# Packing the 88-row remainders of four experts into three full tiles, and writing the gated output over z, in a MoE-Mamba-MoE kernel

## The reference

```
x = x + 0.5 * ffn(layernorm(x))          # FFN 1
x = x + mamba(layernorm(x))              # four Mamba layers, then Wout
x = x + 0.5 * ffn(layernorm(x))          # FFN 2, the same weights

def ffn(xt):                             # 8 experts, 2 of them per token
    topk_w, topk_idx = top_k(xt @ Ws + bs, 2)
    combine = sum(one_hot(topk_idx, 8) * softmax(topk_w))
    g = einsum('td,edf->tef', xt, Wg)    # D = 128, F = 344
    u = einsum('td,edf->tef', xt, Wu)
    y = einsum('tef,efd->ted', silu(g) * u, Wd)
    return einsum('ted,te->td', y, combine)

def mamba_layer(x):                      # 256 channels, 16 states each
    xp, z = split(rmsnorm(x) @ Win)
    xc = silu(causal_conv(xp))           # 4 taps
    dt, B, C = split(xc @ Wx)
    delta = softplus(dt @ Wdt + bdt)
    h[t] = exp(delta[t] * A) * h[t-1] + delta[t] * xc[t] * B[t]
    y = sum_over_states(h * C) + xc * Dp
    return x + (y * silu(z)) @ Wblk
```

## Time and profile before

| | us |
|---|---|
| median of 3 runs | 4566.4 (4564.11 to 4567.35) |
| span of the profiled execution | 4554.2 |
| first core product on POOL | 159.60 |
| last core product on POOL ends | 4402.56 |
| POOL busy | 4093.5 (90%) |
| DVE busy | 4047.9 (89%) |
| PE busy | 3939.2 (86%) |
| ACT busy | 3342.2 (73%) |

### The profile page before, as it was taken

One profiled execution on the slowest core, in us unless ns is written; L12 is line 12 of the kernel. 1 busy time (PEld: TensorE's weight loads), 2 busy tenths in 40 slices (PEclk: granted clock), 3 DMA queues, 4 the chain that ended last, 5 costly groups with the idle time before them and its releaser, 6 DMA issues.

```text
span 4554.2 us, 48397 instructions
## 1 busy us (share of the span) xinstructions
PE 3939.2 (86%) x11712; PEld 1280.3 (28%) x11712; DVE 4047.9 (89%) x5505; ACT 3342.2 (73%) x5047; POOL 4093.5 (90%) x1804
## 2 busy tenths in 40 slices
PE   7886777998999999899998999999899989678769
PEld 2221222232322323232232323223232323122223
DVE  2668898999999999999999999999999999889963
ACT  4566776777777777777778777777777777667734
POOL 0559999999999999999999999999999999999960
PEclk9897887999999999999999999999999999789969
DMA  2233544354434444544454445444444554444410
GB/s 72 61 78 95 115 106 98 85 118 110 97 87 112 107 93 99 114 104 96 98 112 96 97 101 119 95 97 101 112 92 89 117 113 91 101 99 95 99 41 5
DMA packets 154562, 434.46 MB, mean 95 GB/s; under 512 B 16429, under 2 KB 53230, under 8 KB 153903
## 3 DMA queue, kind: packets, MB, share of 16 engines
q1 hardware_dynamic: 154287, 431.36, 41.4%
HBM read 150.28 MB, written 12.58 MB: 36 GB/s over the span
## 4 chain that ended last, share of the span: by engine, by line
POOL 41%; issue 16%; DVE 14%; PE 12%; ACT 8%; DMA 3%; SPq 2%; DVEq 0%; ACTq 0%; POOLq 0%
POOL work L909 21%; POOL work L900 19%; DVE work L720 5%; DVE dA_ps L720 4%; SPq L363 2%; PE d_ps L434 2%; PE s_ps L481 2%; DVE work L725 2%; DMA bc_sb<-bc_rows 2%; ACT sg_sb L583 2%; ACT L583 1%; PE b_ps L427 1%; ACT dA_ps L556 1%; DMA dd_sb<-dd_src 1%; ACT L584 1%
## 5 line engine op out<-in xcount | busy, mean ns | idle before, releaser
L909 POOL TENSOR_TENSOR work<-dd_sb,bc_sb 128x2048 f32<-128x2048 f32 x512 | 2319.6, 4531 | 72.4 <-DMA dd_sb<-dd_src 72.2
L556 ACT ACTIVATE dA_ps<-dd_sb,a_sb 128x512 f32<-128x512 f32 x2048 | 1369.2, 684 | 643.1 <-DVE work L725 542.9
L900 POOL TENSOR_TENSOR work<-work,bc_sb 128x1024 f32<-128x1024 f32 x704 | 1655.9, 2359 | 35.1 <-DVE work L720 34.7
L720 DVE TENSOR_TENSOR_SCAN work<-dA_ps,work 128x512 f32<-128x512 f32 x1408 | 1646.7, 1203 | 40.7 <-POOL work L909 32.0
L720 DVE TENSOR_TENSOR_SCAN dA_ps<-dA_ps,work 128x512 f32<-128x512 f32 x640 | 780.9, 1220 | 10.9 <-ACT dA_ps L556 5.1
L434 PE MATMUL d_ps<-sg_sb,wd_sb 128*128 128x512 f32 (+1 forms) x1536 | 721.0, 601 | 18.8 <-DVE sg_sb L805 18.8
L405 PE MATMUL y_ps<-work,sel_sum 128*32 128x512 f32 x4096 | 580.3, 640 | 81.9 <-POOL work L900 53.7
L421 PE MATMUL a_ps<-xT_sb,wg_sb 128*128 128x512 f32 (+1 forms) x768 | 439.5, 655 | 87.1 <-ACT sg_sb L583 80.7
L421 PE MATMUL b_ps<-xT_sb,wg_sb 128*128 128x512 f32 (+1 forms) x768 | 434.5, 648 | 92.2 <-ACT sg_sb L583 87.8
L725 DVE TENSOR_TENSOR work<-dA_ps,bc_sb 128x512 f32<-128x512 f32 x640 | 435.8, 681 | 8.3
L427 PE MATMUL a_ps<-xs_sb,wu_sb 128*128 128x512 f32 (+1 forms) x768 | 412.2, 619 | 20.7 <-DVE sg_sb L805 16.2
(11 more groups left out here) (116 smaller groups left out, 3823.6 us busy)
## 6 DMA issues: line engine op xcount, KB each, us to landing
dd_sb<-dd_src SPq DMA_DIRECT2D x512, 512.0 KB, 8.5
bc_sb<-bc_rows SPq DMA_DIRECT2D x256, 512.0 KB, 5.8
xr_sb<-in_L_attn_x SPq DMA_DIRECT2D x16, 256.0 KB, 3.3
bc_rows<-dbc_sb SPq DMA_DIRECT2D x128, 32.0 KB, 1.7
x<-xr_sb SPq DMA_DIRECT2D x16, 256.0 KB, 3.6
xr_sb<-x SPq DMA_DIRECT2D x16, 256.0 KB, 2.9
out<-xr_sb SPq DMA_DIRECT2D x16, 256.0 KB, 2.3
wg_sb<-in_L_ffn_Wg SPq DMA_DIRECT2D x1, 1376.0 KB
```

What stands on the lines that cost most here:

```text
L556: act.activation(dA_ps[:, g % NDA, :], dd_sb[:, b, c, 0, :], ACT.Exp, scale=a_sb[:, l, b, j, c:c + 1]).then_inc(dA_ready, 1)
L720: dve.tensor_tensor_scan(dA if on_dve(i) else tile, dA, tile, 0.0, ALU.mult, ALU.add).then_inc(scanned, 1)
L900: pool.tensor_tensor(work[:, g % RING], work[:, g % RING], bc_sb[:, j, 0, :].unsqueeze(1).broadcast_to([128, 2, T]), ALU.mult).then_inc(po ...
L909: pool.tensor_tensor(work[:, g % RING:g % RING + 2].rearrange("p h c t -> p (h c) t"), dd_sb[:, b, :, 1, :], bc_sb[:, j, 1, :].unsqueeze(1 ...
```

## The change

The 88 rows that are left of each expert's F are padded to 96, which is three pieces of 32. The twelve pieces of four experts fill three tiles of 128 rows. A unit so has 22 tiles in place of 24: experts 0 and 4 have two tiles (128, 128), each of the others has three, and the first of the three (`ft == 0`) is a packed one, whose pieces belong to up to two experts (`owner`). A packed u tile is computed by four column strips of 32 rows, each with the gated x of its owner; for this `xs_sb` has two slots. The weights are laid out so on the host, padded with zeros, and Wd comes by one DMA in place of three. `y_sb` is gone: the gated output is written over `zs_sb`. All tables of ticks have new numbers.

```diff
-FT = [(0, 128), (128, 128), (256, 88)]
-NFT = len(FT)
+PACK, PIECE = 4, 32
+NFT, GT = 3, 11
...
-PREP = {"dc1": 79, "dc0": 65, "sq": -15, "ms": -10, "rms": -10, "xn": 2, "xp0": 15, "conv0": 17, "xp1": 25, "conv1": 25,
-        "silu_xc": 27, "z0": 35, "zc0": 27, "z1": 44, "zc1": 43, "silu_z": 59, "wx": 41, "dbc": 40, "rows": 4, "dt0": 48,
-        "sp0": 48, "delta0": 55, "du0": 59, "dt1": 75, "sp1": 72, "delta1": 79, "du1": 82, "dd0": 49, "dd1": 86, "bc": 52}
+PREP = {"dc1": 85, "dc0": 62, "sq": -28, "ms": -8, "rms": -10, "xn": -2, "xp0": 18, "conv0": 13, "xp1": 27, "conv1": 24,
+        "silu_xc": 27, "z0": 95, "zc0": 94, "z1": 114, "zc1": 109, "silu_z": 123, "wx": 43, "dbc": 46, "rows": 42, "dt0": 52,
+        "sp0": 51, "delta0": 59, "du0": 64, "dt1": 66, "sp1": 68, "delta1": 75, "du1": 81, "dd0": 20, "dd1": 99, "bc": 57}
...
+def tiles_of(e):
+
+    return range(0 if e % PACK else 1, NFT)
+
+
+def tiles_until(x):
+
+    return GT * (x // PACK) + max(0, NFT * (x % PACK) - 1)
+
+
+def owner(e, c):
+
+    return e - e % PACK + (4 * (e % PACK - 1) + c) // 3
...
-        y_sb = sb("y_sb", [128, NBLK, T])
-        xs_sb = sb("xs_sb", [128, T])
+        xs_sb = sb("xs_sb", [128, 2, T])
...
-            for dst, src in ((wg_sb[:, :, :], Wg), (wu_sb[:, :, :], Wu), (wd_sb[:, :, 0, :], Wd[0:128]),
-                             (wd_sb[:, :, 1, :], Wd[128:256]), (wd_sb[0:88, :, 2, :], Wd[256:344])):
+            for dst, src in ((wg_sb[:, :, :], Wg), (wu_sb[:, :, :], Wu), (wd_sb[:, :, :], Wd)):
...
-                        pe.wait_ge(xs_ready, E * f + e + 1)
-                        pe.matmul(ps[0:fn, :], wu_sb[:, e, f0:f0 + fn], xs_sb[:, :], start=True, stop=True).then_inc(u_full, 1)
+                        pe.wait_ge(xs_ready, x + 1)
+                        if ft == 0:
+                            for c in range(NG):
+                                last = pe.matmul(ps[PIECE * c:PIECE * (c + 1), :],
+                                                 wu_sb[:, tile_number(e, ft), PIECE * c:PIECE * (c + 1)],
+                                                 xs_sb[:, owner(e, c) % 2, :], start=True, stop=True)
+                            last.then_inc(u_full, 1)
...
-                            act.wait_ge(y_gated, 2 * (before - 1) + b + 1)
+                            act.wait_ge(wblk_full, before)
                         act.activation(zs_sb[:, w % 2, b, :], s_ps[:, :], ACT.Copy).then_inc(z_copied, 1)
...
-                    if k > 0:
-                        dve.wait_ge(wblk_full, k)
-                    dve.tensor_tensor(y_sb[:, b, :], zs_sb[:, par, b, :], y_ps[:, :], ALU.mult).then_inc(y_gated, 1)
+                    dve.tensor_tensor(zs_sb[:, par, b, :], zs_sb[:, par, b, :], y_ps[:, :], ALU.mult).then_inc(y_gated, 1)
...
-                    if xn > 0:
-                        dve.wait_ge(u_full, NFT * xn)
+                    if xn > 1:
+                        dve.wait_ge(u_full, tile_number(xn - 1, 1))
```

More of the change, by code:

```diff
@@ L39 @@
-POST = {"x1": 8, "wblk": 83, "h": 91, "attn": 105, "x2": 105}
-POST_NEAR = {"x1": -65, "wblk": 17, "h": 14, "attn": 35, "x2": 56}
-FFN_AT = {"gb": 5, "xs": 2, "g0": 5, "g1": 10, "g2": 10, "burst": 5, "u0": 10, "u1": 17, "u2": 21, "hh0": 13, "hh1": 16,
-          "hh2": 21, "down": 28}
-START = {"load": -130, "bn": -60, "nb": -44, "xtok": -54, "xt": -38, "xT": -47, "lg": -32, "lg_sb": -35, "mx": -32,
-         "mi": -28, "gap": -17, "we": -31, "eq": -27, "den": -17, "inv": -27, "comb": -13, "ct": -12, "gates": -19}
@@ L45 @@
-END = {"yt": 21, "xo": 32, "bn": 41, "nb": 62, "xtok": 61, "ht": 84, "h": 74, "store": 133, "acc": 10}
+CORE = {"exp": -9, "scan": -1, "dbu": 0, "dve_prod": 0, "pool_prod": 23, "sum": 31, "y0": 87, "y1": 7}
+PREP = {"dc1": 85, "dc0": 62, "sq": -28, "ms": -8, "rms": -10, "xn": -2, "xp0": 18, "conv0": 13, "xp1": 27, "conv1": 24,
+        "silu_xc": 27, "z0": 95, "zc0": 94, "z1": 114, "zc1": 109, "silu_z": 123, "wx": 43, "dbc": 46, "rows": 42, "dt0": 52,
+        "sp0": 51, "delta0": 59, "du0": 64, "dt1": 66, "sp1": 68, "delta1": 75, "du1": 81, "dd0": 20, "dd1": 99, "bc": 57}
@@ L48, in phase_table @@
+FFN_AT = {"gb": 3, "xs": 2, "g0": 4, "g1": 9, "g2": 10, "burst": 5, "u0": 11, "u1": 11, "u2": 22, "hh0": 13, "hh1": 16,
+          "hh2": 21, "down": 32}
+START = {"load": -130, "bn": -62, "nb": -41, "xtok": -46, "xt": -30, "xT": -40, "lg": -30, "lg_sb": -35, "mx": -35,
+         "mi": -35, "gap": -17, "we": -35, "eq": -30, "den": -16, "inv": -28, "comb": -12, "ct": -21, "gates": -19}
+END = {"yt": 28, "xo": 32, "bn": 33, "nb": 71, "xtok": 68, "ht": 78, "h": 73, "store": 133, "acc": 1}
 def phase_table():
@@ L431, in ffn_pe @@
                         pe.wait_ge(acc_ready, f)
-                    for ft, (f0, fn) in enumerate(FT):
-                        pe.wait_ge(hh_ready, NFT * (E * f + e) + ft + 1)
-                        last = pe.matmul(d_ps[:, :], wd_sb[0:fn, e, ft, :], sg_sb[0:fn, ft, :], start=(e == 0 and ft == 0),
+                    for ft in tiles_of(e):
+                        pe.wait_ge(hh_ready, tile_number(E * f + e, ft) + 1)
+                        last = pe.matmul(d_ps[:, :], wd_sb[:, tile_number(e, ft), :], sg_sb[:, ft, :], start=(tile_number(e, ft) == 0),
                                          stop=(e == E - 1 and ft == NFT - 1))
@@ L513, in post_pe @@
                         pe.wait_ge(y_gated, 2 * k + b + 1)
-                        last = pe.matmul(ps[:, :], wblk_sb[:, PHASE[w][1], b, :], y_sb[:, b, :], start=(b == 0), stop=(b == NBLK - 1))
+                        last = pe.matmul(ps[:, :], wblk_sb[:, PHASE[w][1], b, :], zs_sb[:, w % 2, b, :], start=(b == 0), stop=(b == NBLK - 1))
                     last.then_inc(wblk_full, 1)
@@ L563, in burst_act @@
                     return
-                for ft, (f0, fn) in enumerate(FT):
+                for ft in range(NFT):
                     if ft == 2 and at_xc:
@@ L991, in laid_out @@
     name = name.split("_", 2)[2]
-    if name in ("Win", "Wdt", "Wg", "Wu", "Wd"):
+    if name in ("Wg", "Wu", "Wd"):
+        rows = a if name == "Wd" else a.transpose(0, 2, 1)
+        tiles = []
+        for e in range(0, E, PACK):
+            rest = np.zeros((PACK, 3 * PIECE, rows.shape[2]), rows.dtype)
+            rest[:, :F - 256] = rows[e:e + PACK, 256:]
+            rest = rest.reshape(3, 128, -1)
+            for i in range(PACK):
+                tiles += [rest[i - 1]] * (i > 0) + [rows[e + i, 0:128], rows[e + i, 128:256]]
+        return np.stack(tiles).transpose((1, 0, 2) if name == "Wd" else (2, 0, 1))
+    if name in ("Win", "Wdt"):
         return a.transpose(1, 0, 2)
```

68 lines of the change are left out of this document (40 added, 28 removed).

## The result

The changed kernel takes 4593.22 us (4590.53 to 4606.63, 4 runs) against 4566.88 us (4564.11 to 4567.92, 4 runs): a ratio of 1.0064, interval 1.0052 to 1.0076. It is slower by 0.6%; forecast was 4526 and faster. Further down, one execution of e3 (6472.9 us) and one of e7 (12403.1) lie far off; without them the medians there would be 4688.4 and 4569.7.

The account below looks back on a forecast made before the run. POOL was taken to set the pace in the middle, with chains through other engines at the start, near phases and end. Terms -5, -7.5, -16, -6.6 and -5 sum to -40, from 4566.4 to 4526 us; forecast 4510 to 4545, range 4500 to 4562.

Parts of the forecast that it names:

- The start: Weights and first unit: scan weights issued sooner by one Wd transfer, two-tile experts ahead of the first phase; -5 us.
- first two phases: Wx no longer waits behind the two z matmuls and their copies once silu of xc is done; -7.5 us.
- The other near phases: Seven further near waits: same gain at Wx, less a later convolution matmul, 2.6 us each, capped by the wait; -16 us.
- The waits for dd_sb other than the first: Sign for the near phases: POOL's waits for the transfers spreading the prepared phase fall from 31.5 to about 11 us.
- The last units: Final expert chains, POOL out of work: two-tile experts get shorter, packed ones slightly longer; -6.6 us.
- its two terms: Last units: -9.1 us from four two-tile experts, +2.4 from twelve packed tiles at 0.2 each.
- The steady phases: Middle phases paced by POOL: only some waits for DVE's scans can be won back; -5 us (-34.7 to +60).
- A POOL that is full turns none of this into time: Steady phases: work taken from DVE, ACT and PE does not shorten the time; only scans' waits, 34.7 us, can return.
- SP's rows: Steady phases: the rows' store on SP ahead of bc_sb could delay it; slack 1.7 us, expected to cost nothing.
- the slow one: Rival, steady phases: SP's rows make bc_sb late, 55 phases lose 1.1 us each, +60; time 4591; chance 0.10.
- the copy of z holds up ACT: Named way to be wrong: z's copy waits for Wblk, exponentials queue behind it, then DVE's scans; no size or chance.
- the rival: Last units: each packed tile costs 0.65 us, giving -1.3 in place of -6.6; dear strips join a rival of chance 0.12.

Follow-up runs that it names:

- e3: The kernel before with all eight tables of ticks of the changed kernel, no packed tiles: 4688.6 us.
- e7: The changed kernel with each packed u tile as one full matmul in place of four strips (some pieces get a wrong gate): 4571.4 us.
- e12: The kernel before, unchanged, run again for a second profile: time 4563.5 us, span 4561.7.
- e15: The kernel before with Wd loaded by one transfer in place of three, nothing else: 4561.7 us, ratio 0.9991 (0.9981 to 1.0).
- e18: e11 with z ahead of Wx again in the near phases alone: 4671.6 us.
- e4: The kernel before with only the ticks of the z matmuls, their copies and silu of z set late as in the changed kernel: 4830.1 us.
- e5: The changed kernel with the old tables, y_sb kept and one slot of xs_sb (some pieces get a wrong gate): 4555.4 us, ratio 0.9982.
- e11: The changed kernel, new tables and late z, with y_sb kept and one slot of xs_sb (some pieces get a wrong gate): 4601.3 us.
- e17: e5 with strips of two widths in 128 of the 192 packed tiles: 4659.8 us.
- e6: The changed kernel with the old tables but for z's ten numbers, so z is late: 4847.9 us.
- e14: The changed kernel with the projection a window later, the router's transposes ahead and the second z matmul earlier: 4592.9 us.
- e9: The changed kernel with the fourth layer's output projection and the sum that takes it a window later, samples 0 to 12: 4584.3 us.
- e10: e11 with z as early as before the change in the far windows (steady phases) alone: 4673.3 us.
- e2: The changed kernel with the router's transposes and the second z matmul set earlier: 4578.6 us.
- e13: The changed kernel with neighbouring pieces of one owner taken together, giving strips of two widths (64 and 32 columns): 4693.8 us.

## Why the prediction was wrong

**The start: right.** Forecast -5 and -7.5 at the first two phases; measured -12.6 against e12 (-14.8 against the first profile). SP's Wd transfer takes 0.43 in place of 9.24 and xs of the second expert comes 3.8 us sooner (forecast 4). e15 gives 4 us by itself, by an interval that ends at none. Wx starts with silu of xc, by these rows, where it came 4.70 behind it:

```profile
244.56 1.22 ACT L609 ACTIVATE xc_sb<-xc_sb 128x512 f32<-128x512 f32 x2
245.68 1.88 PE L541 MATMUL s_ps<-xc_sb,wx_sb 128*96 128x512 f32 x4
```

**The other near phases: half.** Forecast -16; measured against e12 -6.6 in phases 2 to 5, -1.3 up to phase 9 and -2 in the last ones. The step itself came: in eight of the nine near phases Wx starts 0.0 to 0.6 us ahead of the end of silu of xc, in one 1.5 behind it, where it came 4.2 to 4.7 behind it in all nine. Only half arrived in the time; what became as late is not followed here. The waits for dd_sb other than the first fell from 31.5 to 15.4 (e12: 24.3), forecast was 11. e18 shows that z's place matters there, more strongly than forecast, though in other tables. e4, with z late in the old tables, gains nothing there, so the gain is of z and the rewritten numbers together.

**The last units: right.** Forecast -6.6 (its two terms, -9.1 and +2.4, give -6.7), measured -7.2, 151.6 to 144.4 from the end of the last product (4443.42 + 2.35 to 4590.2). A two-tile expert takes 6.02 us (forecast 6.3), one with a packed tile 8.76 (forecast 8.8), from these rows, where one took 8.56:

```profile
4475.04 0.39 PE L442 MATMUL b_ps<-gates_sb,sel_gate 24*128 24x512 bf16 x1
4483.80 0.39 PE L442 MATMUL a_ps<-gates_sb,sel_gate 24*128 24x512 bf16 x1
4489.82 0.39 PE L442 MATMUL b_ps<-gates_sb,sel_gate 24*128 24x512 bf16 x1
```

**The steady phases: wrong, and this is the step that failed.** The prediction has "A POOL that is full turns none of this into time", a term of -5, and a price for one way to lose alone, SP's rows. It does say that the new tables put other operations ahead of the same scans, but gives this no price. Measured: +58 between phases 9 and 53. That the new tables are the loss, and not the packing, is shown by e5 and e11, which differ in nothing else: from phase 12 to 52 e5 takes 2628.3 us, e12 2626.0, and e11 takes 2680.9:

```profile
973.40:3654.30 2680.90, 2365.67 (x7811) 757.22 (x7810) 2510.96 (x3394) 2046.19 (x3091) 2562.53 (x1122) 0.97 0.44 99
```

Two things were wrong in the step.

First, its one-sidedness. With the old tables, time taken from PE brings nothing there (e5 and e12, with PE busy for 2309 and 2395 us), but a tile that takes 1.0 us more costs 0.8 in the time (e17). A POOL at 98% of a stretch of 261.1 us does not bound alone: it is fed through the chain PE, ACT, DVE. That this chain was about as long as POOL's own work fits these runs, but is argued. A step that is only moved, at no cost in busy time, can then cost as much as one that is added, as e4 and e11 show.

Second, of all that the tables move, z was priced only where it left. The prediction followed it away from Wx, and no row of it asks what stands where it arrives: z0 ahead of the output projection, z1 ahead of the router's transposes and logits, all of them through one bank. The two by two of the runs:

```
                     z early                    z late
old tables      4566.9 (packed: 4555.4*)   4830.1 (packed: 4847.9)
new tables      packed: 4673.3*            4688.6 (packed: 4593.2; 4601.3*)
* y_sb kept, one slot of xs_sb; in 4673.3 z is early in the steady phases alone
```

Late z costs 267 us in the old numbers; the new ones, written around it, win back 142 and, with packing, 255 (e6 to the changed kernel). Packing, with the one Wd transfer in it, is worth 9 us where z is early with the old tables, makes it 18 longer where z is late with them (e6), and is worth 87 to 95 where z is late with the new ones (e3 against e11 and the changed kernel). What remains against the best run with z early is 38 us. In the code the change itself is a reason for a late z: the gated output over z makes the copy of the next z wait for Wblk, and y_sb's room goes to the second gated x. No run has z early and written over, so that z had to be late is not shown. The forecast took the pieces as a sum; the table shows that they are not.

The rivals: the slow one gives 4591, and 4593.2 was measured, but this is luck. Its cause did not appear: SP's rows behind dd0 did not make bc_sb late in the steady phases (one wait for bc_sb, 11.0 us, at the second phase, and e12 has one of 7.4). That the copy of z holds up ACT was named as a way to be wrong, without a chance or price; ACT waits 87.6 us in it (34 times) after 39.3 (62 times), and no run separates this from PE's queue.

**What each part of the 5.3 us per four phases is** was settled in part. It is not the packing (e3, e11) and not the router's own order (e14). The step moves along with the projection when that goes to another window (e9, e14); that it is the projection and z standing together is argued from this.

The clock may be a part. Granted clock in the 10 us from the start of each projection, samples 1 to 12: 1.00 in 11 of 12 before (0.83 in one) and in all 12 of e10; 0.66 or 0.83 in all 12 after, and in 11 of 12 of e3, which has no packed tile. Over the whole stretch from phase 12 to 52, the lower level holds for 37 us in e12 and for 177 after the change. At half the clock, 140 us more are 70 us of PE's work at full clock, an estimate, and the stretch is 53 longer, so in size the clock could be the whole loss. But the time does not follow it: e14 has 106 us at the lower level and is 50 longer than e12, e2 has 85 and is 39 longer, and e17 has 34, less than before, and is 71 longer. No run changes the clock alone, so whether it is a cause or goes with the lateness stays open. So does whether another set of numbers with late z loses nothing.

The rule of the Trainium skill that the prediction weighed ("TensorEngine Tiling (Array Packing)", Key Properties: a change of the tiling mode drains TensorE) has no price with it. The trace agrees where the width changes inside a tile (2.0 against 1.0 us, e13), though it does not part a drain from strips that only wait for each other. At the edge between strips and full matmuls an expert of the last units is 0.2 us longer (8.76 less 8.56), as the sum had it, and not 0.65 as the rival had. In the steady phases the strips were taken for nothing, where full matmuls gave 19 us (e7).

## What to carry to other kernels

When an operation is moved, price the place where it arrives: list what is queued behind it there on each engine and on each shared bank, also if its engine looks less busy than the bound. Where two engines are within a few per cent of a period, test the sensitivity in both directions before trusting "this engine has slack": here, with the old tables, a us less on PE counted 0 and a us more in its tiles 0.8. When a change brings new numbers of order with it, time the new order alone and the change in the old order (as e3 and e5) before adding up the pieces. And a wait that shows in a profile after a change is where the lateness surfaces; take it away once, and see if the time follows, before naming it as the cause.
